# Loading the first expert's weights through GpSimd's queue, and fetching the first tiles before all of the scratch is written

## The reference

```python
W = weights[condition]
y = jnp.einsum('bct,bcd->bdt', x, W)
logits = y @ W_gate + b_gate
_, top_idx = jax.lax.top_k(logits, TOP_K)
y_all = jax.nn.relu(jnp.einsum('bsd,edh->bseh', y, W_e) + b_e)
out = x + jnp.take_along_axis(y_all, top_idx[..., None], axis=2).mean(axis=2)
```

## Time and profile before

| | before |
|---|---|
| median of 3 runs | 971.91 us |
| profiled execution | 978.63 us |
| its span | 976.9 us |
| PE busy | 903.5 us (92%) |
| DVE, ACT, POOL busy | 408.2, 292.9, 495.4 us |
| mean granted clock of PE | 0.96 |
| DMA engines, share over the span | 0.61 |

### The profile page before, as it was taken

One profiled execution on the slowest core, in us unless ns is written; L12 is line 12 of the kernel. 1 busy time (PEld: TensorE's weight loads), 2 busy tenths in 40 slices (PEclk: granted clock), 3 DMA queues, 4 the chain that ended last, 5 costly groups with the idle time before them and its releaser, 6 DMA issues.

```text
span 976.9 us, 16392 instructions
## 1 busy us (share of the span) xinstructions
PE 903.5 (92%) x3988; PEld 708.8 (73%) x3989; DVE 408.2 (42%) x594; ACT 292.9 (30%) x383; POOL 495.4 (51%) x541
## 2 busy tenths in 40 slices
PE   8978886699699799999999999999999999999993
PEld 5534443588588588888888888888888888888882
DVE  3544565333444343633364336333543363333320
ACT  6755552221323221412141214121412231211120
POOL 2053333434453676767556654665566556555411
PEclk9998897799799899999999999999999999999997
DMA  8978898531677655865476447654764465445422
GB/s 315 397 275 306 295 370 303 200 110 48 177 171 187 172 118 105 244 163 122 95 215 162 108 86 216 157 121 91 207 167 110 94 191 118 97 89 102 91 43 43
DMA packets 51391, 163.11 MB, mean 167 GB/s; under 512 B 14178, under 2 KB 14178, under 8 KB 51202
## 3 DMA queue, kind: packets, MB, share of 16 engines
q0 software_dynamic: 25328, 73.59, 35.7%
q1 hardware_dynamic: 19698, 71.84, 20.8%
q10 hardware_dynamic: 6336, 17.34, 4.6%
HBM read 102.28 MB, written 70.94 MB: 177 GB/s over the span
## 4 chain that ended last, share of the span: by engine, by line
PE 77%; DMA 8%; issue 5%; POOL 2%; DVE 2%; ACT 1%; another core or an unknown queue 1%; POOLq 0%; ACTq 0%; SPq 0%; DVEq 0%
PE psO L511 67%; PE psO L448 5%; PE psT L463 3%; DMA rows<-in_x 3%; POOL rows L362 1%; DMA rows<-y_rows,first 1%; DMA y_rows<-ys 1%; DMA out<-ys,idx_s 1%; PE psG L473 1%; PE psG L475 1%; DMA rows<-y_rows,idx_g 1%; DMA out<-rows,first 1%; DMA out<-rows,idx_s 1%; PE psR L486 1%
## 5 line engine op out<-in xcount | busy, mean ns | idle before, releaser
L511 PE MATMUL psO<-w_hi,a_hi 128*128 (+1 forms) x1104 | 343.2, 392 | 15.4 <-DVE a_lo L913 15.4
L511 PE MATMUL psO<-w_lo,a_hi 128*128 (+1 forms) x1104 | 342.2, 391 | 0.0
L511 PE MATMUL psO<-w_hi,a_lo 128*128 (+1 forms) x1104 | 341.4, 390 | 0.0
L362 POOL DMA_INDIRECT rows<-y_rows,idx_g x256 | 266.7, 1042 | 110.2 <-issue 52.4
L511 PEld LDWEIGHTS psO<-w_hi,a_hi 128*128 128x128 f32 x1104 | 207.9, 189 | 59.5 <-issue 16.9
L511 PEld LDWEIGHTS psO<-w_lo,a_hi 128*128 128x128 f32 x1104 | 208.7, 189 | 43.7
L511 PEld LDWEIGHTS psO<-w_hi,a_lo 128*128 128x128 f32 x1104 | 208.5, 189 | 43.8
L913 DVE TENSOR_TENSOR a_lo<-ys,a_hi 128x1024 fp32r<-128x1024 f32 x64 | 78.4, 1225 | 117.3 <-ACT a_hi L677 67.0
L671 ACT ACTIVATE ys<-ys 128x1024 f32<-128x1024 f32 x34 | 36.1, 1061 | 289.3 <-DVE ys L888 253.8
L336 POOL DMA_INDIRECT slot_table<-toks,idx_all x64 | 62.4, 975 | 116.1 <-DVEq L832 98.7
L671 ACT ACTIVATE rows<-rows 128x1024 f32<-128x1024 f32 x35 | 37.1, 1061 | 278.7 <-DVE rows L888 214.5
(11 more groups left out here) (107 smaller groups left out, 433.4 us busy)
## 6 DMA issues: line engine op xcount, KB each, us to landing
raw<-in_L_ffn_W_e SPq DMA_DIRECT2D x64, 512.0 KB, 4.4
rows<-in_x SPq DMA_DIRECT2D x32, 512.0 KB
y_rows<-ys ACTq DMA_DIRECT2D x32, 512.0 KB
out<-rows SPq DMA_DIRECT2D x12, 512.0 KB, 5.6
bias<-in_L_ffn_b_e SPq DMA_DIRECT2D x8, 512.0 KB
rows<-y_rows,idx_g POOLq DMA_INDIRECT x256
slot_table<-toks,idx_all POOLq DMA_INDIRECT x64
raw<-in_L_cond_weights SPq DMA_DIRECT2D x2, 256.0 KB
```

The lines of the kernel that those rows point to most:

```text
L362: pool.indirect_dma_start(out=rows[:, slot, a * DQ:(a + 1) * DQ], out_offset=None, in_=y_parts, in_offset=bass.IndirectOffsetOnAxis(ap=idx ...
L511: last = nc.tensor.matmul(psO[p][:, h * BANK:(h + 1) * BANK], a[:, p, k * P:(k + 1) * P], w[:, bass.ds(slot + (k * H + h * BANK), BANK)], ...
```

## The change

**Weights.** SP's `load_pair` is gone. POOL loads expert 0's eight chunks (`load_first`) into four buffers: the two halves of `raw` and the two halves of `bias`, which the biases need only later. Chunks 0 to 3 are issued at POOL's start, chunks 4 to 7 after `route(1)`, each when its buffer has been split. The splits stand in turns 2, 3, 5 and 6 instead of 2 to 5 (`SPLITS`). SP's load of the first bias, and the ten copies behind it, now wait for all eight splits.

**Zeros at the front.** The scratch has its 128 rows of zeros at its start, and the token n is at row 128 + n. Since `out` keeps its spare rows at the end, DVE computes the destination from the source index (`to_out`, two operations on a tile of indices, done three times). The two stores of zeros are issued at POOL's start.

**First fetches.** `early(t)` reads only the first four groups' part of the scratch (five for tile 3, six for tile 4) and waits for the stores of those groups only. Tile 0's reordering stands on ACT between tiles 30 and 31, and its transposes stand on PE before tile 31's (`place` swaps the two). Tile 1's follow after tile 31's.

**POOL's order.** `route(5)` stands behind `early(1)`. The additions to `out` of tiles 0 and 1 stand ahead of the wait for the indices, and later additions and gathers alternate. On DVE the index work stands ahead of the bias add of tile 2.

```diff
@@ chunks and turns
+        chunk = [raw[:, 0, :], raw[:, 1, :], bias[:, 0:H], bias[:, H:2 * H]]
-        PAIRS = range(1, 1 + KD // 2)
+        SPLITS = {2: 0, 3: 2, 5: 4, 6: 6}
+        def place(n):
+            return {NTILE - 1: NTILE, NTILE: NTILE - 1}.get(n, n)
@@ SyncE
-                def load_pair(j):
-                    if j == 0:
-                        sp.wait_ge(s_fill, 16)
-                    for i in range(2):
-                        k = 2 * j + i
-                        if j:
-                            sp.wait_ge(s_split, k - 1)
-                        sp.dma_start(raw[:, i, :], w_rows[k * P:(k + 1) * P, :]).then_inc(s_raw0[i], 16)
-                    if g in PAIRS:
-                        load_pair(g - PAIRS[0])
+                sp.wait_ge(s_split, KD)
                 load_bias(0)
                 for c in range(len(left)):
                     copy(c)
-                sp.wait_ge(s_spare, 32)
                 sp.wait_ge(s_bias, 16)
                 load_bias(1)
-                sp.wait_ge(s_split, KD)
@@ GpSimd
+                pool.dma_start(y_dram[0:P, :], zero).then_inc(s_spare, 16)
+                pool.dma_start(out[TOK:TOK + P, :], zero).then_inc(s_spare, 16)
+                def load_first(k):
+                    if k == 1:
+                        pool.wait_ge(s_fill, 16)
+                    if k == 3:
+                        pool.wait_ge(s_spare, 32)
+                    if k >= RAW:
+                        pool.wait_ge(s_split, k - RAW + 1)
+                    pool.dma_start(chunk[k % RAW], w_rows[k * P:(k + 1) * P, :]).then_inc(s_raw0[k % RAW], 16)
@@ early(t)
+                    upto = max(t + 2, NG - 4)
                     if t == 0:
                         pool.wait_ge(s_spare, 32)
-                        for s in range(G):
-                            pool.wait_ge(s_yout[s], 16 * NG)
+                    for s in range(G):
+                        pool.wait_ge(s_yout[s], 16 * upto)
...
-                        out=rows[:, t % 2, :], out_offset=None, in_=y_dram,
+                        out=rows[:, t % 2, :], out_offset=None, in_=y_dram[0:P + upto * G * P, :],
@@ ScalarE, turn(g)
-                        act.dma_start(y_dram[n * P:(n + 1) * P, :], ys[:, s, :]).then_inc(s_yout[s], 16)
+                        act.dma_start(y_dram[P + n * P:P + (n + 1) * P, :], ys[:, s, :]).then_inc(s_yout[s], 16)
...
+                        if n == NTILE - 2:
+                            unfold(0)
@@ VectorE
+                def to_out(to, src, empty):
+                    own(V.tensor_scalar(empty, src, float(P), float(TOK + P), ALU.is_lt, ALU.mult))
+                    own(V.scalar_tensor_tensor(to, src, -float(P), empty, ALU.add, ALU.add))
```

More of the change, by code:

```diff
@@ L88, in build @@
         first = sb("first", [P, EARLY], U32)
+        first_to = sb("first_to", [P, EARLY], U32)
+        behind = sb("behind", [P, EARLY])
         part_q = sb("part_q", [P, 1])
@@ L175, in build @@
         s_yout = [sem(f"s_yout{i}") for i in range(G)]
-        s_raw0 = [sem(f"s_raw0{i}") for i in range(2)]
+        s_raw0 = [sem(f"s_raw0{i}") for i in range(RAW)]
         s_raw = [sem(f"s_raw{i}") for i in range(RAW)]
@@ L389, in scatter @@
                         in_=o_sb[m], in_offset=None, compute_op=ALU.add).then_inc(s_add, 16)
+                for k in range(RAW):
+                    load_first(k)
                 route(0)
-                pool.dma_start(y_dram[TOK:TOK + P, :], zero).then_inc(s_spare, 16)
                 route(1)
-                pool.dma_start(out[TOK:TOK + P, :], zero).then_inc(s_spare, 16)
+                for k in range(RAW, KD):
+                    load_first(k)
                 route(2)
@@ L397, in _ @@
                 route(4)
-                route(5)
                 early(0)
                 early(1)
+                route(5)
                 early(2)
@@ L405, in _ @@
                 early(4)
-                pool.wait_ge(s_idx, 1)
-                for t in (EARLY, EARLY + 1):
-                    pool.wait_ge(s_un, t - 1)
-                    gather(tile(0, t))
-                regather(tile(0, 7))
                 for j in range(2):
@@ L416, in _ @@
                 scatter_early(0)
+                scatter_early(1)
+                pool.wait_ge(s_idx, 1)
+                for t in (EARLY, EARLY + 1):
+                    pool.wait_ge(s_un, t - 1)
+                    gather(tile(0, t))
+                scatter_early(2)
+                regather(tile(0, 7))
+                scatter_early(3)
                 regather(tile(0, 8))
-                scatter_early(1)
+                scatter_early(4)
                 regather(tile(0, 9))
-                scatter_early(2)
-                scatter_early(3)
+                scatter(tile(0, 5))
                 regather(tile(0, 10))
-                scatter_early(4)
-                scatter(tile(0, 5))
+                scatter(tile(0, 6))
                 regather(tile(0, 11))
-                scatter(tile(0, 6))
                 scatter(tile(0, 7))
@@ L452, in transposes @@
                 def transposes(n):
+                    at = place(n)
                     if n < NTILE:
@@ L561, in _ @@
                 ranks(NG - 2)
-                transposes(NTILE)
                 transposes(NTILE + 1)
@@ L920, in _ @@
                 slots(NG - 2)
-                low(NTILE)
                 low(NTILE + 1)
+                dve.wait_ge(s_first[0], 16 * Q)
+                to_out(first_to[:, 0:EARLY - 2], first[:, 0:EARLY - 2], behind[:, 0:EARLY - 2])
+                dve.sem_inc(s_to, 1)
                 logits(NG - 1)
@@ L932, in _ @@
                 low(NTILE + 3)
-                finish_early(2)
-                low(NTILE + 4)
+                for c in range(3, EARLY):
+                    dve.wait_ge(s_first[c - 2], 16 * Q)
+                to_out(first_to[:, EARLY - 2:EARLY], first[:, EARLY - 2:EARLY], behind[:, EARLY - 2:EARLY])
+                dve.sem_inc(s_to, 1)
                 dve.wait_ge(s_tab, Q * 16)
```

73 lines of the change are left out of this document (40 added, 33 removed).

## The result

| | before | changed kernel |
|---|---|---|
| median of the runs, us | 971.54 (4 runs, 964.79 to 973.25) | 923.86 (4 runs, 923.56 to 925.36) |
| profiled execution: time, span, us | 978.63, 976.9 | 923.56, 921.8 |
| granted clock, mean | 0.963 | 0.987 |
| tile 30's product starts (piece A) | 140.00 | 123.72 |
| from there to the first large product (piece B) | 43.3 | 23.3 |

The ratio is 0.9525 with a 95% interval of 0.9478 to 0.9571: faster. A later sitting (a sitting is a set of runs taken together on one chip) gave 0.9523 (0.9452 to 0.9594). The medians differ by only 47.7 us, since the traced execution of the kernel before took 7.1 us more than its median. Which piece holds these 7 us is not known, so the sizes of the pieces are those of this pair of traces.

A forecast was written before the change was run, and what follows sets the result against it. From 339.73 us TensorE's large matmuls run without a gap, so only the waits before that could shrink. Gains of 17 + 18 + 19 = 54 us off a median of 971.91 gave 918 us, range 904 to 941.

The forecast's parts named there:

- Piece A: First stage up to tile 30's product: with SP no longer waiting for splits, a gain of 17 us (10 to 23).
- The two deductions: In Piece A, taken off 22.8 us: 4 for the early load, 2 for excess in turns 3 to 5.
- The loss of 7 us: In Piece A, by the rule of queues served in turns: slower `x` loads cost 7 us in place of 4.
- Piece B: Tile 30's product to the first large product: early fetches shorten 43.3 us to 25, a gain of 18 (7 to 23).
- 3 beyond cover and 2 of slow matmuls: In Piece B: 3 us of first fetch beyond TensorE's other work, 2 us for matmuls at the lower clock.
- Piece C: First large product to 339.73 us: of 22.2 us of waits and slow clock, 19 go (0 to 22).
- The sum: Whole kernel: 17 + 18 + 19 = 54 us, giving 924.6 on the profiled time, 917.9 off the median.
- 1, copies as the wait: Late copies delay the first additions and gathers, so TensorE idles again from the first large product; 937 us, chance 0.17.
- 2, bound by bytes: First stage limited by its 45 MB, so the freed queue only shifts waits; 935 us, chance 0.17.
- 3, slower: Additions ahead of the first gather delay every gather on POOL if copies end past 240; 993 us, chance 0.02.
- 4, fetches not early: The first fetch still ends up behind the last stores, leaving 36 to 43 us there; 933 us, chance 0.12.
- Signs: Things the new trace should show in TensorE's waits, turns 3 to 5, both product starts and tile 4's bias add.

The follow-up runs named there:

- only_weights: The kernel before with only the weights part added: expert 0's chunks on GpSimd's queue, bias and copies behind the eight splits; 956.38 us, ratio 0.984.
- weights_on_sync: The changed kernel with expert 0's weights back on SyncE's queue in pairs, with its waits for the splits; 945.84 us, ratio 0.973.
- copies_first_2: Repeat, beside the changed kernel, of the changed kernel with four of ten copies ahead of SyncE's wait for the splits; 931.76 us, ratio 0.9586.
- no_reorder: The changed kernel with GpSimd's old order of additions and gathers and VectorE's old place for the index work; 942.69 us, ratio 0.9697.
- spread_loads_2: Repeat, beside the changed kernel, of the changed kernel with GpSimd's early DMAs spread over the products of tiles 5 to 10; 926.27 us, ratio 0.9522.
- spread_loads: The changed kernel with GpSimd's early DMAs (zeros, chunks 0 to 3) issued one by one after the products of tiles 5 to 10; 948.34 us, ratio 0.9695.
- copies_first: The changed kernel with the first four of ten copies issued ahead of SyncE's wait for the eight splits; 950.06 us, ratio 0.972.

## Why the prediction was right

I predicted 918 us (904 to 941), and the median was 923.86.

**Piece A** was 17 us and measured 16.3. The two deductions were both mis-sized. The early load took 5.4 us, not 4 (tile 6's product 1.2 us later, turns 1 and 2 together 4.2 longer: 60.36 - 25.32 against 30.81). Turns 3 to 5 took 47.5 us where I had 46.5 and a loss of 2, so that was 1. Of the 5.4 us only the 4.2 in turn 1 are clear: that turn took 15.2 us in each of the four traces without the early load and 16.5 to 19.5 in the eight with it, while tile 6's product started anywhere from 24.14 to 26.43 without it. The cause of the gain is shown: the weights part alone moves tile 30's product by 17.0 us (only_weights), and outside sitting 2 that product starts at 122.3 to 124.9 in all traces with the part and at 138.4 in the one that takes it out (weights_on_sync).

The Trainium skill's rule on queues served in turns ("DMA: Bandwidth & Descriptors", "Queues, rings and completion order") agrees with this trace in the shares. From 10 to 30 us GpSimd's, SyncE's and ScalarE's queues had 38.0, 37.1 and 27.3% of the 16 engines (q0, q1 and q10 below: packets, MB, share), and SyncE's moved 3.04 MB where it had moved 4.87 before:

```profile
q0 software_dynamic: 857, 3.11, 38.0%
q1 hardware_dynamic: 837, 3.04, 37.1%
q10 hardware_dynamic: 719, 2.21, 27.3%
```

The loss of 7 us that I worked out from it does not follow, though. Its 2.7 us per tile are those of turn 0; in turn 1 a tile took 3.8 us before, so a load every 3.9 us would have cost next to nothing there, and that is where the clear loss lies, with 4.9 us per tile.

**Piece B** was 18 us and measured 19.9. ACT waited 4.4 us for the first fetch; the sum had 3 beyond cover and 2 of slow matmuls, and TensorE's own two waits were 1.94 and 0.96. My picture of B left one thing out: 6.6 us of its gain come with the weights part alone (only_weights). I had put them down to the fetches. That the copies' place in time does it is shown for the changed kernel by copies_first_2, and inferred for only_weights. That the fetch came so soon was not forecast either: it landed 4.9 us after its issue (127.14 to 132.03), where I had a median of 8.4.

**Piece C** was 19 us and measured 18.9 to the end of the span. The wait of 10.5 us for tile 0's addition and the three waits for `a_lo` are gone. One 1.93 us gap remains, for tile 4's fetch, which I had not named. One detail was wrong: I expected the first gather about 35 us behind the first large product; it came at 45.6. I had left out that the index work reads the whole table, and that read landed only at 187.5, 40.5 us behind the first large product; moving the work ahead of tile 2's bias add brought its end forward by only 3.9 us (43.7 us behind the first large product, 47.6 in no_reorder). The second addition, which waited 9.48 us for the first one's landing, had ended before the index work did (189.40 against 190.74), so it is not what held the gather. The late gather cost TensorE nothing.

**The sum.** On the profiled execution's own time I had 54 us, and 55.1 was measured (924.6 against 923.56). The step that missed is the last one, where I took another 6.7 us off. I treated that execution's distance from its median as an offset that the changed kernel would share. It is a spread that belongs to the kernel before: its untraced runs in five sittings lie between 964.5 and 984.6 us, while the changed kernel's eight runs in two sittings lie within 923.6 to 927.0. What makes the kernel before vary stays open. No one part holds the spread: in the sitting where the kernel before ranged over 14.8 us, the four kernels with only one or two of the three parts of the change ranged over 2.5 to 3.2 each. That its three traced executions all lie above their medians may also mean that tracing adds time to it. That A came out within 1 us is partly luck: one error of 1.4 us and one of 1 us in the other direction cancel.

**Rivals.** 1, copies as the wait: not in the changed kernel (first addition at 176.75, bias add of tile 4 at 208.31), though its contention is real where copies meet a fetch. 2, bound by bytes: true only while the early load moves, up to 40 us and in spread_loads_2 up to 60, where spreading the same bytes gained nothing. From 60 us on turns take 15.8 us with TensorE all but fully busy, though the DMA engines (shares of 0.96 to 1.02 from 60 to 120 us) then have little to spare. 3, slower: the copies would have had to end past 240, and their issue ended at 166. 4, fetches not early: B would have stayed at 36 to 43, and it did so only where the fetches were taken out (36.9).

**Signs.** TensorE has no wait for `rows<-in_x` after 40 us (the last one, of 2.24, ends at 36.70), turns 3 to 5 take near 16, tile 30's product is at 123.72 against 123 and the first large product at 147.06 against 148, and there is no gap over 2 us after that: all as written.

## What to carry to other kernels

Look for an ordered queue in which a transfer with a long wait stands ahead of ones that others need. Moving eight loads to another engine's queue gave 17 us with the bytes unchanged, although the crowding at the start cost 4 to 5 us. Look also at what a bulk transfer with no deadline runs beside. Here its best place was between the fetches that TensorE waits for: ten copies cost 5.8 us when four of them moved ahead of the first fetch, and 3 to 5 us when they ran into the fifth. And do not carry a profiled execution's distance from its median over to the changed kernel; make the sum on the profiled time and stop there.

## What the runs showed of the hardware

With three queues busy from 10 to 40 us the DMA engines moved 419 GB/s, but a 512 KB load on GpSimd's queue took far longer to land than the weights had on SyncE's. The page's DMA issues (count, KB, median us from issue to landing) of the changed kernel:

```profile
raw<-in_L_ffn_W_e SPq DMA_DIRECT2D x56, 512.0 KB, 6.0
...
raw<-in_L_ffn_W_e POOLq DMA_DIRECT2D x4, 512.0 KB, 12.2
bias<-in_L_ffn_W_e POOLq DMA_DIRECT2D x4, 512.0 KB, 15.0
```

The other 56 weight loads of this kernel landed in 6.0 us, all 64 of the kernel before in 4.4. Half of GpSimd's eight were issued at 9 to 19 us (12.7 and 15.0 us to landing), the others at 79 to 83 us (10.4 and 15.3), where the engines are full too. Up to 130 us ACT has no wait for any of the eight, while TensorE did wait for `x` loads that took 10 to 11 us.

In sitting 2, spread_loads and copies_first took 948.34 and 950.06 us, in sitting 3, on another chip, 926.27 and 931.76. Their slow turns show late hand-overs between ScalarE, VectorE and TensorE at the same places in both kernels (2.64 us in spread_loads, 2.62 in copies_first), with DMA shares of 0.79 and 0.81 from 100 to 120 us. The kernel before did not slow down in sitting 2 (975.62 against 973.79), and the changed kernel was not run in it, so whether it shares this is open, and so is the cause.
